# A two-layer recurrence on one core: the loop of eight slots becomes one of four, with the projections copied by ScalarE and a third tile of layer 0 multiplied in bf16 parts

## What is computed

```
def layer(x, h0, Wx, Wh, b):
    xW = einsum('ntd,dh->nth', x, Wx) + b          # the projection
    step: h = tanh(h_prev @ Wh + xw_t)             # 1024 steps, each needs the one before
x = x + layer(x, cond_1024, L0_Wx, L0_Wh, L0_b)    # x is 8 x 1024 x 512, float32
x = x + layer(x, cond_1024, L1_Wx, L1_Wh, L1_b)
```

## Time and profile before

| | |
|---|---|
| median of 3 runs | 2059.51 us (2058.35 to 2059.56) |
| the profiled execution, span | 2057.6 us |
| TensorE busy | 2044.6 us, 99% |
| VectorE busy | 1746.3 us, 85% |
| ScalarE busy | 1280.9 us, 62% |
| GpSimd busy | 444.9 us, 22% |
| granted TensorE clock | 1.000 |

### The profile page before, as it was taken

How to read it: one execution, slowest core, us unless ns; L and a number is a source line. 1 busy time by engine, 2 the same in 40 slices (tenths; PEclk the granted TensorE clock), 3 DMA queues, 4 the chain that set the end, 5 groups by cost and what they waited for, 6 DMA issues and landing times.

```text
span 2057.6 us, 219078 instructions
## 1 busy us (share of the span) xinstructions
PE 2044.6 (99%) x98388; PEld 1863.8 (91%) x98388; DVE 1746.3 (85%) x10221; ACT 1280.9 (62%) x6660; POOL 444.9 (22%) x2054
## 2 busy tenths in 40 slices
PE   8999999999999999999999999999999999999999
PEld 6999999999999999999999999999999999999997
DVE  5888888888888888888888888888888888888887
ACT  4666666666666666666666666666666666666665
POOL 3222222222222222222222222222222222222221
DMA  3000000000000000000000000000000000000000
GB/s 108 25 26 25 26 25 26 25 26 25 27 24 27 24 28 24 28 24 28 24 27 24 27 24 27 24 27 24 28 23 28 23 27 24 27 24 27 24 27 15
DMA packets 111960, 56.33 MB, mean 27 GB/s; under 512 B 12432, under 2 KB 111008, under 8 KB 111520
## 3 DMA queue, kind: packets, MB, share of 16 engines
q1 hardware_dynamic: 111168, 53.53, 8.8%
q10 hardware_dynamic: 576, 1.18, 0.2%
q0 software_dynamic: 32, 0.02, 0.0%
HBM read 37.90 MB, written 16.78 MB: 27 GB/s over the span
## 4 chain that ended last, share of the span: by engine, by line
PE 99%; DMA 1%; issue 0%; DVE 0%; ACT 0%; SPq 0%; ACTq 0%
PE ps_rec L270 44%; PE ps_rec L287 33%; PE ps_xw L247 22%; DMA wx<-wx_in 0%; DMA wh<-wh_in 0%; PE ps_rec L339 0%; DVE zt L463 0%; ACT h L387 0%; SPq L223 0%; ACTq L421 0%; ACTq L420 0%; DVE z L472 0%; DVE x_out L503 0%; SPq L222 0%
## 5 line engine op out<-in xcount | busy, mean ns | idle before, releaser
L270 PE MATMUL ps_rec<-wh,h 128*32 128x128 f32 x33024 | 1261.2, 273 | 3.3 <-ACT h L387 2.8
L387 ACT ACTIVATE h<-z 128x24 f32<-128x24 f32 x4066 | 654.7, 208 | 666.4 <-DVE z L472 625.0
L287 PE MATMUL ps_rec<-wh_part,h 128*32 128x128 bf16 x48792 | 1036.9, 219 | 1.5 <-issue 1.5
L270 PEld LDWEIGHTS ps_rec<-wh,h 128*32 128x32 f32 x33024 | 880.0, 109 | 30.1 <-ACT h L387 6.7
L287 PEld LDWEIGHTS ps_rec<-wh_part,h 128*32 128x32 bf16 x48792 | 724.0, 96 | 151.1 <-issue 1.8
L205 POOL TENSOR_TENSOR h<-h 128x16 f32<-128x16 f32 x2032 | 430.6, 212 | 1589.9 <-DVE h L205 1589.9
L472 DVE TENSOR_REDUCE z<-zt 128x24 f32<-128x72 f32 x4066 | 664.5, 205 | 69.7 <-DVE zt L463 0.6
L376 ACT ACTIVATE ps_rec<-ps_xw,mask 128x128 f32<-128x128 f32 x2048 | 664.2, 324 | 77.9 <-PE ps_xw L247 77.9
L463 DVE STREAM_TRANSPOSE zt<-ps_rec 128x128 f32<-128x128 f32 (+1 forms) x2063 | 649.8, 316 | 18.7 <-PE ps_rec L270 12.7
L205 DVE TENSOR_TENSOR h<-h 128x16 f32<-128x16 f32 x2034 | 356.0, 175 | 209.2 <-ACT h L387 0.2
L247 PE MATMUL ps_xw<-wx,x_pe 128*32 128x128 f32 x8248 | 404.6, 273 | 2.0 <-issue 1.1
(11 more groups left out here) (20 smaller groups left out, 16.5 us busy)
## 6 DMA issues: line engine op xcount, KB each, us to landing
x_pe<-x_t SPq DMA_DIRECT2D x256, 64.0 KB, 2.0
x_dve<-x_t SPq DMA_DIRECT2D x256, 64.0 KB, 1.9
out_t<-x_out SPq DMA_DIRECT2D x256, 64.0 KB, 1.5
wh<-wh_in SPq DMA_DIRECT2D x1, 1024.0 KB, 5.7
wx<-wx_in SPq DMA_DIRECT2D x1, 1024.0 KB, 8.3
wx<-wx_in ACTq DMA_DIRECT2D x1, 512.0 KB, 5.2
wx<-wx_in SPq DMA_DIRECT2D x1, 512.0 KB, 5.0
wh<-wh_in SPq DMA_DIRECT2D x1, 512.0 KB, 7.2
```

What stands on the lines that cost most here:

```text
L270: mm = pe.matmul(rows(ps_rec[l][n % 2], g), h_step(l, n - 1)[:, k, :], wh[l][:, k, g * P:(g + 1) * P], start=False, stop=k == KC - 1 and n ...
L287: mm = pe.matmul(rows(ps_rec[l][n % 2], g), h_bits(l, n - 1)[:, k, :], wh_part[l][:, i, at:at + P], start=False, stop=k == KB[l] - 1 and i ...
L387: act.activation(h_of(l, n)[:, tiles, :], src[:, tiles, :], ACT.Tanh).then_inc(h_count(l, n)[0], 1)
```

## The change

- **Three tiles of layer 0 in parts.** `KB` becomes (3, 2): tile 2 of layer 0 goes from 8 float32 instructions to 12 bf16 ones. TensorE waits for the rests of tiles 0 and 1 ahead of the parts and for those of tile 2 after 24 of the 36 instructions.
- **Rests.** In layer 0 VectorE makes both rests of tiles 0 and 1, one after the other, with a semaphore between them. GpSimd makes both rests of layer 0's tile 2 (128 x 8) and both of layer 1's tiles 0 and 1; it waits for ScalarE's tanh instead of VectorE's first rest.
- **Halves.** The transpose and the sums go in two halves of two tiles each, in all steps (before: one transpose; the sums in tiles 0 to 2 and tile 3). TensorE's float32 tile 3 of layer 0 and tiles 2 and 3 of layer 1 wait for the second half.
- **Copies on ScalarE.** One PSUM bank collects each layer's projections. ScalarE copies it to SBUF (`xw`) when it is full, `begin` reads the copy, and the bank is seeded again. Layer 1's projections read a copy of `x_mid` (`xm_pe`), which ScalarE makes once in four slots (`pass_xm`); TensorE waits for it with `xm_done`. In all, three more 128 x 128 ScalarE instructions in four slots. Layer 0's `x` for the projections has one buffer after the start.
- **Uneven projections.** A slot's first place holds one and a half tiles, the second half a tile (64 columns). For this, tiles 0 and 2 of each projection are cut into two halves of 64 columns.
- **A loop of four slots** (`RING` = 4, eight before); the lag of seven steps stays. ScalarE's order in a slot is written anew.

In the diff `projection` is TensorE's, `pass_xm` and the `slot` after it are ScalarE's, the two loops over (l, k) and over `ORDER` are GpSimd's, and `rests` is VectorE's.

```diff
-KB = (2, 2)
+KB = (3, 2)
-RING = 8
+RING = 4
+PAIR = 2
+LAG = 7
+WIDE, LOW, HIGH = slice(0, P), slice(0, SIDE), slice(SIDE, P)
+PROJECT = ((0, ((2, HIGH), (3, WIDE)), 1, ((0, LOW),)), (1, ((0, HIGH), (1, WIDE)), 1, ((2, LOW),)),
+           (1, ((2, HIGH), (3, WIDE)), 0, ((0, LOW),)), (0, ((0, HIGH), (1, WIDE)), 0, ((2, LOW),)))
...
             def projection(s, half):
...
+                    if pieces[0] == (0, LOW) and l == 1:
+                        pe.wait_ge(xm_done, 1)
+                    for k, cols in pieces:
+                        project(l, c, k, cols)
...
+            def pass_xm(c):
+
+                act.wait_ge(mid_done, c + 1)
+                if c:
+                    act.wait_ge(proj_done[1], c)
+                act.activation(xm_pe[:, :], x_mid[c % 2][:, :], ACT.Copy).then_inc(xm_done, 1)
...
             def slot(s):
...
+                r, t = s // S4, s % S4
+                if s < T:
+                    tanh(0, s)
+                if t == 0 and 0 <= r - 1 < NG:
+                    pass_xm(r - 1)
+                if t == 1 and 3 <= r + 1 < NG + 1:
+                    act.sem_inc(seed0_done, -1)
+                if t == 2 and 0 <= r - 1 < NG:
+                    act.sem_inc(xm_done, -1)
+                    copy(1, r - 1)
+                if (n := number(1, s + 1)) is not None:
+                    begin(1, n)
+                if t == 3 and 1 <= r < NG:
+                    act.wait_ge(copied[1], copy_count(1, r - 1))
+                    seed(1, r)
+                if (n := number(1, s)) is not None:
+                    tanh(1, n)
...
+                if 2 <= s + 2 < T:
+                    begin(0, s + 2)
+                if t == 0 and 2 <= r + 1 < NG:
+                    copy(0, r + 1)
...
+            for l, k in ((0, 0), (0, 1), (1, 0), (1, 1), (0, 2)):
...
             for l, n in ORDER:
                 if is_split(l, n):
-                    pool.wait_ge(rest_done[l], n + 1 if l else n + 2 - PARTED)
-                    rest(pool, l, n, 2).then_inc(split_count(l, n)[0], S4 if (l, n) == (0, PARTED - 1) else 1)
+                    mine, done = (rest_done[1], n + 1) if l else (late_done, n + 2 - PARTED)
+                    tiles = HALVES[0] if l else slice(2, 3)
+                    pool.wait_ge(*h_count(l, n, 1 - l))
+                    rest(pool, l, n, 1, tiles).then_inc(mine, 1)
+                    pool.wait_ge(mine, done)
+                    rest(pool, l, n, 2, tiles).then_inc(split_count(l, n, 1 - l)[0], PAIR if (l, n) == (0, PARTED - 1) else 1)
...
-                for tiles in HALVES if is_whole(l, n) else (slice(0, KC),):
+                for tiles in HALVES:
...
+            def rests(n):
+                if is_split(0, n):
+                    dve.wait_ge(*h_count(0, n, 0))
+                    rest(dve, 0, n, 1).then_inc(rest_done[0], 1)
+                    dve.wait_ge(rest_done[0], n + 2 - PARTED)
+                    rest(dve, 0, n, 2).then_inc(split_count(0, n, 0)[0], PAIR if n == PARTED - 1 else 1)
```

More of the change, by code:

```diff
@@ L88, in build @@
                                      for name in ("x_pe", "x_dve", "x_mid", "x_out"))
-        ps_xw = [[psum(f"ps_xw{l}_{i}") for i in range(2)] for l in LAYERS]
+        xm_pe = sb("xm_pe", [P, GRP])
+        xw = [[sb(f"xw{l}_{i}", [P, P]) for i in range(2 - l)] for l in LAYERS]
+        ps_xw = [[psum(f"ps_xw{l}_{i}") for i in range(2 - l)] for l in LAYERS]
         ps_rec = [[psum(f"ps_rec{l}_{i}") for i in range(2)] for l in LAYERS]
@@ L200, in x_of, with rest @@
             return xs[n // S4 % 2][:, :].rearrange("p (k s b) -> p s k b", s=S4, b=B)[:, n % S4]
-        def rest(eng, l, n, part):
-            step, to, of, tiles = h_step(l, n), h_cols(n, part), h_cols(n, part - 1), slice(0, KB[l])
+        def rest(eng, l, n, part, tiles=HALVES[0]):
+            step, to, of = h_step(l, n), h_cols(n, part), h_cols(n, part - 1)
             return eng.tensor_tensor(step[:, tiles, to], step[:, tiles, of], h_bits(l, n)[:, tiles, of], ALU.subtract)
@@ L241, in rows, with project @@
                 return bank[32 * g:32 * g + 32, 0:P]
-            def project(l, c, k):
-                src = (x_mid if l else x_pe)[c % 2][:, k * ROWS:(k + 1) * ROWS]
+            def project(l, c, k, cols=WIDE):
+                src = xm_pe if l else x_pe[c == 1]
                 for g in range(QG):
-                    mm = pe.matmul(rows(ps_xw[l][c % 2], g), src, wx[l][:, k, g * P:(g + 1) * P], start=False,
-                                   stop=False, skip_group_check=True, tile_position=(0, 32 * g))
+                    mm = pe.matmul(rows(ps_xw[l][l == 0 and c == 1], g)[:, cols], src[:, k * ROWS:(k + 1) * ROWS],
+                                   wx[l][:, k, g * P:(g + 1) * P][:, cols], start=False, stop=False,
+                                   skip_group_check=True, tile_position=(0, 32 * g))
                 if k == KC - 1:
@@ L315, in slot @@
                     pe.wait_ge(x_first[1], DMA)
-                    for k in range(KC - 1):
-                        project(0, 1, k)
+                    for k, cols in ((0, WIDE), (1, WIDE), (2, LOW)):
+                        project(0, 1, k, cols)
                 projection(s, 0)
@@ L329, in slot @@
                     recur_whole(0, s + 1)
-            def turn(r):
-                for s in range(RING * r, RING * (r + 1)):
-                    slot(s)
             def warm(bank, rounds):
@@ L356, in _ @@
             recur_whole(0, 0)
-            for r in range(FIRST):
-                turn(r)
+            for s in range(PARTED):
+                slot(s)
             pe.wait_ge(s_wpart[0], PARTS * KB[0])
-            with pe.Fori(0, AFTER - FIRST, 1):
-                turn(FIRST)
-            turn(AFTER)
+            with pe.Fori(0, (T - PARTED) // RING, 1):
+                for s in range(PARTED, PARTED + RING):
+                    slot(s)
+            for s in range(T, T + LAG):
+                slot(s)
         @block.scalar
@@ L428, in _ @@
                 act.wait_ge(s_bias[l], DMA)
-                for c in range(2):
+                for c in range(2 - l):
                     seed(l, c).then_inc(s_seed, 1)
```

192 lines of the change are left out of this document (93 added, 99 removed).

## The result

The changed kernel takes 2152.68 us (median of 4 runs, 2152.31 to 2153.25); the kernel before takes 2059.28 (2058.35 to 2059.56) on the same chip. The ratio is 1.0455, 95% interval 1.044 to 1.047. The forecast was 2147. The granted clock is full in both, so nothing of the difference comes from it.

A forecast was written before the change was run, and what follows sets the result against it. TensorE's work and layer 0's chain were equally long, 1.980 us a slot; afterwards the chain binds. Three slots of 2.015 and one of 2.22 average 2.066, adding 87 us over 1016 slots: 2147, range 2080 to 2210.

The forecast's parts named there:

- Layer 0's chain in ordinary slots: Layer 0's steps from parts to next parts, in three slots of four: 1.975 us summed, 2.015 with two surcharges.
- TensorE's late start: Layer 0's parts on TensorE after a wait: 24 instructions take 0.55 us from their load instead of 0.53, so 0.02 more.
- The loop head: The place behind TensorE's loop branch, once in four slots; the prediction gave it no cost.
- The wait for `xm_done`: TensorE waits for ScalarE's `x_mid` copy before the half projection tile, once in four slots; that slot costs 2.22 us.
- GpSimd beside VectorE: GpSimd's first third-tile operation runs alongside VectorE's second rest: bounds 0 and 0.055 us, 0.02 taken.
- the rival of full exclusion: GpSimd's operation holds VectorE's second rest in full: ordinary slots 2.05 us, 2174 in all; chance 0.24.
- Half-wide float32 tiles: TensorE's projection tiles of 64 columns: 0.11 us taken for a half tile, bounds 0.11 and 0.22.
- the rival that had them cost a whole tile: Half-wide float32 projection tiles on TensorE take a whole tile's time: mean slot 2.185 us, 2268 in all; chance 0.06.
- ScalarE to GpSimd: Handoff from tanh to GpSimd's rests, taken as 0.08 us; rival: 0.15 dearer than from VectorE, 2202, chance 0.08.
- Faster, since only TensorE's work counts: Rival: TensorE's work alone sets the pace, ordinary slots of 1.934 us, 2013 in all; chance 0.05.
- The signs named beforehand: Changed profile: TensorE under 97% busy, load waits of 0.2 to 0.25 us for VectorE's second rest and `xm_pe`, slot lengths.
- the `xm` slot: The one slot in four where TensorE waits for `xm_done`: forecast 2.22 us, 2.15 to 2.3 as a sign.

The follow-up runs named there:

- experiment 2: The changed kernel with TensorE's loop begun behind layer 0's parts instead of ahead of them, same order and work: 2119.80 us.
- experiment 5: The changed kernel with ScalarE's `x_mid` copy ahead of layer 0's tanh and TensorE's branch between layer 1's float32 tiles and its parts: 2061.11 us.
- experiment 1: The changed kernel with ScalarE's copy of `x_mid` put ahead of layer 0's two tanh instead of behind them: 2089.11 us.
- experiment 9: experiment 5 without GpSimd's two rests of layer 0's third tile, so part of the computation is missing: 2041.22 us.
- experiment 6: The kernel before with only the third tile of layer 0 in parts (`KB` = (3, 2)) and what that needs: 2251.09 us.
- experiment 7: The changed kernel without GpSimd's two rests of layer 0's third tile, so part of the computation is missing: 2153.02 us.

## Why the prediction was right

The forecast of 2147 missed the 2152.7 by 0.3%. Its two main steps, layer 0's chain as the bound and the wait for the copy, are what the runs show. That it came so close is partly luck: two terms were off and nearly cancel, and a third had the right size for a wrong reason. With the head's cost taken away, in experiment 2, the kernel takes 2120, 27 less than the forecast.

- *Layer 0's chain in ordinary slots*: 2.015 predicted, 1.963 and 1.982 measured. Each step by the trace, from start to start over the turns: parts to transpose 0.74 (0.73 predicted), transpose to sum 0.304 (0.30), sum to tanh 0.223 (0.24), tanh to rest 0.247 (0.25), rest to rest 0.21 (0.21), the second rest 0.196, and from its end to the load 0.053. Most steps held. Three are mis-sized by 0.01 to 0.02 each: sum to tanh; the second rest and the handoff behind it, 0.249 together, where the forecast had 0.245 and 0.02 for GpSimd; and TensorE's late start, priced at 0.02, of which parts to transpose shows 0.01. Three such slots (the last without the head's 0.077) are 0.12 us a turn shorter than forecast, x 254 turns 31 us.
- *The loop head*: priced at nothing. The change halves the turn of the loop; the list of its parts has that edit, but the prediction worked out no cost for it. Behind the branch the load comes 0.130 after the rest's end instead of 0.053, and the parts take 0.540 from first to last instead of 0.468: 0.077 + 0.067 (the transpose comes 0.806 after the parts' start instead of 0.74) = 0.144 us a turn, and x 254 turns 37 us. 37 less the 31 of the term above are the 6 us between forecast and measurement. Experiment 2 gained 33 us of it by moving the branch, experiment 5 28 us against experiment 1. This is the step that was missing. The kernel before has such branches too, half as many, and the earlier trace rows show no cost: there TensorE still had work queued, now its wait has emptied the queue.
- *The wait for `xm_done`*: its working held: 0.79 from transpose to copy, a copy of 0.293 (0.28 predicted), 0.05 to the load, 0.36 to the next parts. The slot measured 2.292 against 2.22, and the 0.07 are the head's drawn-out parts (2.226 in experiment 2, without them). Its removal gave 64 us.
- *GpSimd beside VectorE*: 0.02 taken, 0.021 measured on the second rest, 0.020 a slot in experiment 9. The size is right and its reason is not: the prediction took it that so short an operation holds the other up for a part of its row only. The Trainium skill (SBUF — State Buffer, section "Who interferes with whom") lets one instruction hold the other for its whole length. The trace agrees: the second rest ends 0.027 after GpSimd's operation, whether it starts 0.03 or 0.05 behind that operation's start. So the rival of full exclusion had the mechanism and only its price wrong. It took 0.05 from GpSimd's end to VectorE's, read from an operation of 32 columns; with 16 it is 0.027. GpSimd's operation lasts 0.202, the rest starts 0.033 after it and would last 0.175 alone: 0.202 + 0.027 - 0.033 - 0.175 = 0.021 late, and not 0.055. Its time of 2174 is out.
- *Half-wide float32 tiles*: 8 instructions of 64 columns take 0.11 to 0.12 us from start to start, as taken from the earlier trace rows; the rival that had them cost a whole tile is out.
- *ScalarE to GpSimd*: 0.08, no dearer than from VectorE; that rival is out too.
- *Faster, since only TensorE's work counts*: out by experiment 5, in which it had its best chance and came out level. The chain is 1.977, not the 1.934 of TensorE's work.
- *The signs named beforehand*: `xm_pe` among the waits with 0.25, 254 times (right); the `xm` slot between 2.15 and 2.3 (right, 2.29) and the others between 1.95 and 2.05 (right, the one at the head a hair over); TensorE under 97% busy (wrong, 98%; waits of 0.2 us may be too short to pull down a busy time whose ends are modelled, which no run shows); the wait for VectorE in three slots of four (listed for the head alone, 250 times; in the others the gap is 0.12 and the list doesn't name it).

## What to carry to other kernels

Where an engine's work and a chain of dependences are equally long, ask of every edit which of the two it shortens: here one was shortened and the other kept, and the best that could be made of the change is the old time. A wait in front of an in-order queue costs its full length to all that stands behind it, even once in four slots, and where the producer stands in its own engine's order can be most of it (64 us for two lines). Put a loop's branch behind long work whose waits are over, look at the price of each turn again whenever the queue ahead of it may be empty, and count the instructions of the body before unrolling further. Where two engines touch SBUF at once, look at when the held instruction ends, and not only at how much longer it gets.

## What the hardware showed that I had not expected

- A TensorE loop body of 1728 matmuls and loads was fetched anew each turn, 148 KB of it, and the kernel took 3958 us instead of 2153; bodies of 1600 (experiment 6), 1536 (the kernel before) and 864 weren't.
- A compare and branch of TensorE took 0.208 us, and the next load started 0.055 after its end. Where the queue was empty, TensorE's loads stood still for 0.17; behind 16 float32 matmuls with all waits over it cost nothing that shows (slots of 1.977 with and without it).
- Matmuls right behind such a branch can be drawn out: 36 of them took 0.540 us from first to last in the changed kernel, 0.51 in experiment 1 and 0.58 in experiment 7, 0.468 elsewhere. The branch alone isn't the cause, as in experiment 6 the parts right behind it took 0.468; by what mechanism isn't settled.
- A VectorE subtraction with both inputs in SBUF that started 0.03 us after one of GpSimd was held until 0.027 us after GpSimd's end: 0.196 instead of 0.175.
- ScalarE's `begin` with a mask takes 356 ns when it reads SBUF (2040 times) and 324 when it reads PSUM (2048 times, in the kernel before). In this kernel that was hidden.
